# A decoder layer's last chunk: its four feed-forward products issued in a row, and transposes with more places

## The reference

```python
x = x + attention(layernorm(x))
x = x + cross_attention(layernorm(x), ctx)
y = layernorm(x)
h = y @ ternary(W_fc).T          # 256 -> 1024
h = gelu(h)                      # exact gelu
h = layernorm(h) * ln_w + ln_b   # over the 1024
x = x + h @ ternary(W_proj).T    # 1024 -> 256
```

## Time and profile before

| | us |
|---|---|
| median of 3 runs | 1205.69 |
| lowest and highest | 1205.24 and 1211.36 |
| profiled execution | 1210.68 |
| its span on the core | 1208.6 |

### The profile page before, as it was taken

One profiled execution on the slowest core, in us unless ns is written; L12 is line 12 of the kernel. 1 busy time (PEld: TensorE's weight loads), 2 busy tenths in 40 slices (PEclk: granted clock), 3 DMA queues, 4 the chain that ended last, 5 costly groups with the idle time before them and its releaser, 6 DMA issues.

```text
span 1208.6 us, 18959 instructions
## 1 busy us (share of the span) xinstructions
PE 1153.4 (95%) x6476; PEld 590.3 (49%) x6476; DVE 1046.1 (87%) x1974; ACT 862.6 (71%) x1898; POOL 296.2 (25%) x403
## 2 busy tenths in 40 slices
PE   6989999999999999999999999998799999999995
PEld 4544333333333333333333333334467778767775
DVE  4688799999999999999999999746699899998875
ACT  4322588888888888888888888746578778777852
POOL 2224010110111011011101000013665446545421
PEclk9999899999999999999999999979999999999998
DMA  4777112750331233033124000112211121000001
GB/s 168 241 233 244 54 33 37 148 115 9 63 59 29 40 60 56 12 63 59 32 38 68 7 7 11 38 33 85 79 38 48 41 71 51 20 18 18 2 17 36
DMA packets 45920, 74.99 MB, mean 62 GB/s; under 512 B 10112, under 2 KB 23808, under 8 KB 45824
## 3 DMA queue, kind: packets, MB, share of 16 engines
q0 software_dynamic: 9648, 27.27, 13.1%
q1 hardware_dynamic: 36176, 46.50, 12.7%
HBM read 47.53 MB, written 25.69 MB: 61 GB/s over the span
## 4 chain that ended last, share of the span: by engine, by line
PE 82%; DVE 5%; ACT 4%; issue 4%; POOL 2%; DMA 1%; SPq 1%; DVEq 0%; ACTq 0%; POOLq 0%
PE ps L1382 21%; PE ps L1369 21%; PE ps L1227 15%; PE ps L1264 10%; PE ps L1549 4%; PE ps L1469 3%; PE ps L1534 2%; PE ps L1478 2%; ACT prob L630 2%; ACT ot L681 1%; PE ps L1488 1%; DVE xhat L1120 1%; DVE maxes L857 1%; PE ps L1412 1%; DMA Ks<-qk_scratch 1%
## 5 line engine op out<-in xcount | busy, mean ns | idle before, releaser
L864 DVE TENSOR_REDUCE maxes<-ps 128x1 f32<-128x512 f32 x968 | 607.3, 683 | 36.3 <-PE ps L1264 19.0
L630 ACT ACTIVATE prob<-ps 128x512 f32<-128x512 f32 x1024 | 531.9, 604 | 134.3 <-PE ps L1369 133.1
L1369 PE MATMUL ps<-Qs,Ks 50*128 50x512 f32 x1024 | 381.9, 455 | 9.9 <-ACT prob L630 5.3
L1369 PEld LDWEIGHTS ps<-Qs,Ks 50*128 50x128 f32 x1024 | 170.1, 186 | 324.1 <-ACT prob L630 307.8
L1264 PE MATMUL ps<-Ks,Qs 48*128 48x512 f32 x1024 | 319.3, 430 | 2.7 <-DVE maxes L857 2.6
L1382 PE MATMUL ps<-prob,V_all 128*32 128x512 f32 x2048 | 276.3, 612 | 0.8 <-ACT prob L630 0.8
L1264 PEld LDWEIGHTS ps<-Ks,Qs 48*128 48x128 f32 x1024 | 167.1, 186 | 45.2 <-DVE maxes L857 16.2
L340 POOL DMA_DIRECT2D Qs<-qk_scratch x90 | 44.4, 500 | 469.2 <-PE ps L1382 469.0
L702 ACT ACTIVATE pe_<-ps,nmx 128x64 f32<-128x64 f32 x512 | 109.3, 365 | 7.3 <-DVE nmx L1039 7.3
L549 POOL TENSOR_TENSOR pe_<-pe_,rsum 128x512 f32<-128x512 f32 x64 | 66.6, 1050 | 51.9 <-DVE rsum L1056 51.9
L1549 PE MATMUL ps<-t_p,fT 128*128 128x256 f32 x512 | 77.8, 295 | 0.0
(11 more groups left out here) (115 smaller groups left out, 1241.0 us busy)
## 6 DMA issues: line engine op xcount, KB each, us to landing
qk_scratch<-parts SPq DMA_DIRECT2D x32, 512.0 KB, 5.4
Qs<-qk_scratch POOLq DMA_DIRECT2D x90, 128.0 KB, 5.3
Ks<-qk_scratch POOLq DMA_DIRECT2D x90, 128.0 KB, 7.6
o_scratch<-ot SPq DMA_DIRECT2D x128, 32.0 KB
on_raw<-o_scratch SPq DMA_DIRECT2D x8, 512.0 KB
r_raw<-r_scratch SPq DMA_DIRECT2D x16, 256.0 KB
x_in<-in_x SPq DMA_DIRECT2D x8, 512.0 KB, 4.0
out<-xo SPq DMA_DIRECT2D x8, 512.0 KB, 2.8
```

Source lines behind the costliest of these rows:

```text
L630: act.activation(prob[:, U % 2, j // 2, j % 2, :], ps[:, n % ST_BANKS, :], ACT.Exp).then_inc(exp_done, 1)
L864: dve.tensor_reduce(maxes[:, qc, j * BLK + blk, half:half + 1], ps[:, MAX_BANK["tile", t], :], AX.X, ALU.max).then_inc(max_reduced, 1)
L1369: pe.matmul(ps[:, n % ST_BANKS, :], stack(Ks[g], j, ROWS, slice(kb * P, (kb + 1) * P)), stack(Qs[g], j, ROWS, slice(qc * CH, (qc + 1) * CH ...
```

## The change

- TensorE's tail issues `fc(END, 0..3)` with only the transposes of tiles 6 and 7 of chunk END-1 between them. `f_proj(END - 1, 4..7)` stand behind all four, in a row.
- The gelus of blocks 2 and 3 of chunk END write into `pe_`, the probabilities' tile, which nobody uses any more, and wait no longer for blocks 0 and 1 to be normalised (`gl_tile`).
- Chunk END-1 uses all four places of `fT` (it still has two banks to transpose into).
- VectorE's `f_out(END - 1)` moves from the middle of the normalisation of chunk END to behind it, and statistics and normalisations are interleaved in another order.
- GpSimd's `x2_plus_b(END)` moves from behind the four `rstd_f(END)` to ahead of them, behind `x2_apply(END)`.

```diff
-    return ((4, 5, 0, 1)[t % 4], t % 4) if c == END else (4 + t % 2, t % 2)
+    return (4, 5, 0, 1)[t % 4] if c == END else 4 + t % 2, t % 4 if c >= END - 1 else t % 2
...
+        def gl_tile(c, blk):
+
+            if c == END and blk >= 2:
+                return pe_[:, 2 * (blk - 2):2 * (blk - 1), :].rearrange("p a q -> p (a q)")
+            return gl[:, blk % 2, :]
...
             rstd_3(END)
+            pool.wait_ge(xn3_ready, NCH)
+            x2_plus_b(END)
             for blk in range(BLK):
                 rstd_f(END, blk)
-            x2_plus_b(END)
...
-                if n >= 2:
+                if n >= 2 and not (c == END and blk >= 2):
                     act.wait_ge(xhat_done, n - 1)
...
-                if c == END and t >= 4:
+                if c == END or c == END - 1 and t >= 4:
                     act.wait_ge(fp_done, n - 3)
-                elif n >= 2 and not (c == END and t >= 2):
+                elif n >= 2 and not (c == END - 1 and t >= 2):
                     act.wait_ge(fp_done, n - 1)
...
             f_transpose(END - 1, 5)
             f_proj(END - 1, 3)
+            fc(END, 0)
             f_transpose(END - 1, 6)
-            f_proj(END - 1, 4)
-            fc(END, 0)
+            fc(END, 1)
             f_transpose(END - 1, 7)
-            f_proj(END - 1, 5)
-            fc(END, 1)
-            f_proj(END - 1, 6)
-            f_proj(END - 1, 7)
             fc(END, 2)
             fc(END, 3)
+            for t in range(4, HT):
+                f_proj(END - 1, t)
```

More of the change, by code:

```diff
@@ L736, in gelu @@
                 act.wait_ge(fc_done, n + 1)
-                if n >= 2:
+                if n >= 2 and not (c == END and blk >= 2):
                     act.wait_ge(xhat_done, n - 1)
                 r = fc_bank(c, blk)
-                act.activation(gl[:, blk % 2, :], ps[:, r:r + 2, :].rearrange("p a q -> p (a q)"),
+                act.activation(gl_tile(c, blk), ps[:, r:r + 2, :].rearrange("p a q -> p (a q)"),
                                ACT.Gelu).then_inc(gelu_done, 1)
@@ L800, in _ @@
             ft_high(END - 1, 5)
+            gelu(END, 0)
             ft_high(END - 1, 6)
-            gelu(END, 0)
+            gelu(END, 1)
             ft_high(END - 1, 7)
-            for blk in range(1, BLK):
-                gelu(END, blk)
+            gelu(END, 2)
+            gelu(END, 3)
             for t in range(HT):
@@ L1106, in f_stats @@
                 for h in range(2):
-                    i = dve.bn_stats(fstats[:, k, h, :], gl[:, k, h * 512:(h + 1) * 512])
+                    i = dve.bn_stats(fstats[:, k, h, :], gl_tile(c, blk)[:, h * 512:(h + 1) * 512])
                 i.then_inc(fstats_done, 1)
@@ L1119, in f_apply @@
                     dve.wait_ge(hT_done, HT * c)
-                dve.tensor_scalar(xhat[:, blk, :], gl[:, k, :], fmv[:, k, 0:1], frstd[:, k:k + 1],
+                dve.tensor_scalar(xhat[:, blk, :], gl_tile(c, blk), fmv[:, k, 0:1], frstd[:, k:k + 1],
                                   ALU.subtract, ALU.mult).then_inc(xhat_done, 1)
@@ L1208, in _ @@
             ft_low(END - 1, 5)
+            f_stats(END, 0)
             ft_low(END - 1, 6)
-            f_stats(END, 0)
+            f_stats(END, 1)
             ft_low(END - 1, 7)
-            f_stats(END, 1)
             f_apply(END, 0)
+            f_stats(END, 2)
             f_apply(END, 1)
-            f_out(END - 1)
-            f_stats(END, 2)
             f_stats(END, 3)
@@ L1219, in _ @@
             f_apply(END, 3)
+            f_out(END - 1)
             for t in range(HT):
```

## The result

Of 20 executions each, the changed kernel has a median of 1205.99 us (1198.43 to 1209.1) and the kernel before 1212.45 (1201.82 to 1215.44). The ratio is 0.9942, with a 95% interval from 0.9923 to 0.9962: 7.0 us faster by the ratio, between 4.6 and 9.3 (the two medians themselves lie 6.5 apart). The forecast of the gain, 7.3, lies in that interval, but so does the 5.97 that the tail of the profile gained, and in the tail the clock did not do what the forecast had assumed: that 7.0 is so near 7.3 is in part luck. Executions of either kernel don't lie around one value; what spreads them is part of the result, and the second half of the experiments is about it.

The account below looks back on a forecast made before the run. The tail was taken as bound by a chain of ScalarE, VectorE and GpSimd, not TensorE. Gains 1.04 + 1.00 + 1.21 + 2.02 + 2.07 = 7.3 us gave 1205.69 - 7.3 = 1198.4, range 1197.2 to 1203.5.

Parts of the forecast that it names:

- (a): Tail, start of the first `fc`: it waits only for `x3_low` and starts at 1170.76; gain 1.04 us.
- (b): Tail, first `fc` to the statistics of block 1: 5.32 instead of 6.32 us; gain 1.00.
- (c): Tail, statistics of block 1 to the start of the fourth normalisation: 8.11 instead of 9.32 us; gain 1.21.
- (d): Tail, fourth normalisation to chunk END's transposes: 0.86 instead of 2.88 us, with `x2_plus_b` long over; gain 2.02.
- (e): Tail, chunk END's transposes to `f_out(END)`: 11.68 instead of 13.75 us if the clock holds; gain 2.07.
- that rival: Tail: VectorE is held beside the moved `x2_plus_b`, losing 1.1 or 2.1 us; 1199.5 to 1200.5 us, chance 0.07.
- The collision in (c): Tail: GpSimd's root for block 1 holds VectorE's normalisation 0; taken as 0.05 us, bounds 0 and 0.3.
- the likeliest case: Tail: TensorE's clock holds through the shortened wait, the full 7.3 us is gained; 1198.4 us, chance 0.48.
- the first rival: Tail: the clock falls all the same after TensorE's 2.1 us wait; gain 5.3, about 1200.4 us, chance 0.33.
- the slower rival: Tail: the clock falls and stays at half to the end; kernel ends at 1208.4 us, chance 0.03.

Follow-up runs that it names:

- pool_alone: Kernel before with only GpSimd's `x2_plus_b(END)` moved ahead of its four roots; median 1210.99 us, ratio 0.9995 to the kernel before.
- before_filled: Kernel before with 28 unread matmuls in TensorE's wait ahead of the last chunk's transposes; median 1210.74 us, ratio 0.9998 to the kernel before.
- after_filled: Changed kernel with 9 unread matmuls in TensorE's wait ahead of the last chunk's transposes; median 1204.51 us, ratio 0.995 to the kernel before.
- attn_fill1: Changed kernel with one unread matmul in each of the last 11 attention steps; median 1198.62 us, ratio 0.9887 to the kernel before.
- attn_fill2: Changed kernel with two unread matmuls in each of the last 11 attention steps; median 1200.97 us, ratio 0.9906 to the kernel before.
- after_attn_fill1: Changed kernel with one unread matmul in each of the last 11 attention steps, rerun in another group; median 1199.28 us, ratio 0.989 to the kernel before.
- early_transposes: Changed kernel, transposing three blocks of the last chunk's first four tiles before the last normalisation; median 1204.94 us, ratio 0.9936 to the kernel before.

## Why the prediction was right, and where it was wrong

Term by term, in the two profiles:

| term | forecast | measured | what the rows show |
|---|---|---|---|
| (a) start of the first `fc` | 1.04 | 1.02 | 10.08 behind the tail's first transpose instead of 11.10 |
| (b) to the statistics of block 1 | 1.00 | 0.81 | 1179.51 - 1174.00 = 5.51 |
| (c) to the fourth normalisation | 1.21 | 1.32 | 1187.51 - 1179.51 = 8.00 |
| (d) to the transposes | 2.02 | 2.01 | 0.81 instead of 2.82 |
| (e) to the output addition | 2.07 | 0.81 | 12.94 |
| sum | 7.3 | 5.97 | |

(a) and (d) were right, and (c) within 0.11. In (b) the first `fc` starts TensorE from a short wait and keeps it 0.1 longer than the sisters from which it was costed, 1175.97 - 1174.00 = 1.97 to the next transpose, so that the second `fc` starts 0.12 later behind the first than costed. The second gelu follows 2.12 instead of 2.06 behind it, and VectorE starts its statistics later by both. VectorE was not held at the new place of `x2_plus_b`; that rival is out by two traces, this one and pool_alone's. The collision in (c) cost VectorE nothing. It cost GpSimd 0.47 that nobody waited for.

In (e) the likeliest case did not come in the profile, and the first rival did, in the form of a shorter stretch, for which the prediction left between 5.3 and 6.5: behind a wait of 2.08 the clock fell, but for less of the work than before. The prediction had said of itself that it is wrong as a whole if the clock falls. before_filled and after_filled show that its size had been worked out right, and that the clock is all of it. How often it falls across executions can't be seen, since only profiled ones give stretches; among the four kernels with the changed tail and nothing in its wait (changed, attn_fill1, attn_fill2, after_attn_fill1) it took 12.90 to 12.97 each time, so the chance of 0.48 for a clock that holds was too high.

So term (e) was too large by 1.26, and the rest of the sum by 0.1. The step that failed by most is the one from the profile to the time: "that execution was 5.0 over the median, with nothing in the tail that would explain it, so I carry the gain over to the median". Two things were wrong there. The median of three executions was taken as the kernel's, where twenty had 1212.45 and the lowest and highest already lay 6 us apart. And the explanation was in the rows: the stretch from 796.2 to 809.7 at a clock of 0.50 was used there as the longest one seen, to cost the slower rival, and not asked what it costs where it stands. There it costs 5.6 us, and 8 together with the one near 823, of the 9 between the two groups. A range that reached from the lowest to the highest execution shown, less the gain, would have been 1198 to 1204, and three executions seldom hold the extremes: it had to go past both.

What stays open is why the second stretch, near 823, comes in some executions only, and what decides the 2 to 5 us by which even the kernels with extra matmuls per step differ. For the latter the traces show a part. Ahead of 780 the thirteen profiles have between 6.8 and 17 us at half clock, near 63, 120 and 130. They come to `abs_sum` at 791.75 to 793.91 with 6.8, at 793.07 to 795.36 with 10.2, at 796.23 and 796.37 with 13.6, and at 798.49 with 17. The 3.22 by which the changed kernel's profile comes late to the tail are of the same kind: 0.86 are there at `abs_sum`, and 2.4 come with the stretch near 823, all in code that the change does not touch.

## What to carry to other kernels

Where a list of work for the last tiles is bound by a chain over three engines, cost it as distances between starts along the chain: put the products in a row so that what feeds the chain comes first, keep what has time (the projections, the output, the residual) behind it, and look for an addition on GpSimd beside a VectorE operation that is recorded with three times its length. Ahead of a forecast of some 0.5% look at the granted clock over the whole span, not only where the change is: a stretch at half clock in a stage that nobody touches can be worth more than the change. Where such a stretch follows short waits in every step, a matmul that nobody reads may be the cheapest edit of all; here 11 of them took 5 to 7 us off, about as much as the whole rewriting of the tail. What such a stretch costs is read from the trace, between two groups of instructions that both kernels have, far more closely than from a few executions.

## What the runs showed of the hardware

- The clock of TensorE fell to 0.50 near 796 without any long wait: in the 7 us ahead of it TensorE was busy for 6.09 of them in the kernel before and for 6.54 in the changed one, with waits of 0.45. With one matmul more per step, and 6.43 busy of 7, it stayed at 1.00. So the busy time recorded here doesn't tell by itself on which side a stage lies.
- A wait of 2.08 us behind solid work was followed by half clock in each of the four profiles that have it; in all four the clock stood at 1.00 to the end of the wait and fell between 0 and 1.2 us behind the start of the transposes. A wait of 0.65, the 16 transposes and a wait of 1.24 were not followed by it (early_transposes).
- Half clock cost far less than its length: in the tail 3.4 us of it took 1.1 us of time, near 796 13.65 us of it took 5.6. The Trainium skill, TensorE: Matmul & The Clock Gate, section "Part 1: The HAM clock gate", puts the penalty of the clock's ramp below 1% of a typical kernel's span. By these runs the difference between the two groups alone is about 0.75% (9 of 1206); that is below 1%, and more than the change's own 0.58%. What all stretches at half clock cost together no run shows.
- GpSimd's root, recorded from 1181.45, took 1.02 instead of 0.55, while VectorE's normalisation, recorded from 1181.64, took its usual 0.80. The Trainium skill, SBUF — State Buffer, section "Who interferes with whom", gives the shared ports to whoever issues first and makes the other wait. Here the one that was recorded first waited; its operand accesses may have come later than the start of its record, which no run here shows.
